# Projection and heads of a decoder layer: more q and k transfers in flight, and the first half of v issued from ScalarE's queue

## What is computed

```python
xn = _rms(x, g1)
Q = jnp.einsum('bsf,ef->bse', xn, Wq).reshape(b, s_len, H, HD)   # H = HD = 16
K, V = ...                                                        # likewise
pQ, pK = jax.nn.elu(Q), jax.nn.elu(K)
kv1 = jnp.einsum('bshe,bshd->bsed', K1, V) * SCALE
w1 = jnp.einsum('bshe,bsed->bshd', Q1, kv1)      # and w2 from the second halves
attn = w1 - lmb * w2
```

## Time and profile before

| what | value |
|---|---|
| time, median of 3 | 799.29 us (796.55 to 799.43) |
| the profiled execution | 796.2 us, its span 794.5 us |
| loop of projection and heads | about 40 to 249 us of the span |
| PE busy | 661.5 us (83%) |
| DVE, ACT, POOL busy | 494.8, 357.6, 331.8 us |

### The profile page before, as it was taken

How to read it: one execution, slowest core, us unless ns; L and a number is a source line. 1 busy time by engine, 2 the same in 40 slices (tenths; PEclk the granted TensorE clock), 3 DMA queues, 4 the chain that set the end, 5 groups by cost and what they waited for, 6 DMA issues and landing times.

```text
span 794.5 us, 22042 instructions
## 1 busy us (share of the span) xinstructions
PE 661.5 (83%) x8346; PEld 612.4 (77%) x8346; DVE 494.8 (62%) x1239; ACT 357.6 (45%) x814; POOL 331.8 (42%) x393
## 2 busy tenths in 40 slices
PE   4569879788957266766567999999999999999998
PEld 4447767576746155666447999999999999999997
DVE  4645543455421478777447877777777777777763
ACT  4343335343423344344235555555545555554432
POOL 0021110111101988887243555464555445455222
PEclk8798989898978577777858999999999999999999
DMA  8334444345332132333200011011111001110000
GB/s 267 33 61 95 101 103 121 75 121 122 92 88 83 53 106 94 115 107 100 82 20 21 21 35 34 2 35 33 33 33 33 26 7 33 33 33 14 15 14 27
DMA packets 84136, 50.08 MB, mean 63 GB/s; under 512 B 31320, under 2 KB 83808, under 8 KB 84064
## 3 DMA queue, kind: packets, MB, share of 16 engines
q1 hardware_dynamic: 84064, 49.07, 22.7%
HBM read 23.88 MB, written 12.58 MB: 46 GB/s over the span
## 4 chain that ended last, share of the span: by engine, by line
PE 48%; SPq 14%; issue 12%; DVE 10%; DMA 9%; POOL 4%; ACT 2%; POOLq 0%; DVEq 0%; ACTq 0%
PE banks L618 42%; SPq L534 9%; DMA h_qk<-p_qk 7%; PE banks L671 3%; SPq L519 2%; POOL f_hT_lo L1705 1%; DVE m_t L1374 1%; POOL m_rh L1615 1%; DVE m_at L1367 1%; DMA n_gw<-in_L_ffn_gate_w_dram 1%; DVE m_n L1361 1%; PE banks L755 1%; PE banks L781 1%; DVE m_a L1382 1%; POOL m_r L1615 1%
## 5 line engine op out<-in xcount | busy, mean ns | idle before, releaser
L1705 POOL TENSOR_TENSOR f_hT_lo<-f_hs,f_hT_hi 128x512 fp32r<-128x512 f32 x64 | 87.2, 1363 | 103.2 <-ACT f_hT_hi L1198 103.2
L1615 POOL TENSOR_TENSOR m_rh<-m_ms,mhalf 128x32 f32<-128x32 f32 x16 | 88.3, 5521 | 1.3
L1567 DVE SCALAR_TENSOR_TENSOR f_hs<-banks,nbic,f_h 128x256 f32<-128x256 f32 x128 | 54.5, 478 | 43.2 <-PE banks L618 43.2
L618 PE MATMUL banks<-woT_hi,f_hT_lo 128*128 128x256 f32 x256 | 74.5, 291 | 0.2 <-POOL f_hT_lo L1705 0.2
L618 PE MATMUL banks<-f_adT_hi,lbT_lo 128*128 128x256 f32 x256 | 72.9, 285 | 0.0
L618 PE MATMUL banks<-woT_lo,f_hT_hi 128*128 128x256 f32 x256 | 71.9, 281 | 0.0
L618 PE MATMUL banks<-woT_hi,f_hT_hi 128*128 128x256 f32 x256 | 71.7, 280 | 0.0
L618 PE MATMUL banks<-f_xT_hi,wiT_lo 128*128 128x256 f32 x256 | 71.6, 280 | 0.0
L618 PE MATMUL banks<-f_xT_lo,wiT_hi 128*128 128x256 f32 x256 | 71.6, 280 | 0.0
L618 PE MATMUL banks<-f_xT_hi,wiT_hi 128*128 128x256 f32 x256 | 71.5, 279 | 0.0
L618 PE MATMUL banks<-f_adT_lo,lbT_hi 128*128 128x256 f32 x256 | 71.5, 279 | 0.0
(11 more groups left out here) (261 smaller groups left out, 2093.4 us busy)
## 6 DMA issues: line engine op xcount, KB each, us to landing
h_qk<-p_qk SPq DMA_DIRECT2D x64, 128.0 KB, 3.7
xin<-in_x_dram SPq DMA_DIRECT2D x16, 256.0 KB, 3.6
h_v<-p_v SPq DMA_DIRECT2D x128, 32.0 KB
attn_scratch<-h_wn SPq DMA_DIRECT2D x16, 256.0 KB, 2.2
m_w<-attn_scratch SPq DMA_DIRECT2D x16, 256.0 KB, 2.7
m_x<-in_x_dram SPq DMA_DIRECT2D x16, 256.0 KB, 2.9
x_scratch<-m_y SPq DMA_DIRECT2D x16, 256.0 KB, 2.2
c_x<-x_scratch SPq DMA_DIRECT2D x16, 256.0 KB, 2.7
```

Of the source, the lines that this page charges most:

```text
L618: ins = pe.matmul(acc, left(a), right(b), start=first and n == 0, stop=last and n == 2, skip_group_check=skip)
L1567: ins = dve.scalar_tensor_tensor(out=f_hs[:, j % 2, c * T:(c + 1) * T], in0=bank[HB[j]][:, c * T:(c + 1) * T], scalar=nbic[:, f:f + 1], in ...
L1615: pool.tensor_tensor(out_ap, tmp, mhalf[:, 0:width], ALU.pow).then_inc(done, 1)
L1705: pool.tensor_tensor(lo, f_hs[:, j % 2], hi.bitcast(F32), ALU.subtract).then_inc(f_hlo, 1)
```

## The change

Three edits. The limit on q and k transfers in flight is gone. The first half of v (b = 0) is issued from ScalarE's queue, in the new stage `values_out`: four transfers between the first and the second pair of Relu and Exp, and four behind the last pair. SyncE's list is put in another order: the second half of v stands between the two halves of the input, the eight q and k transfers stand in two groups of four, and one of the two stores stands behind each group.

```diff
@@ tiles_in @@
-                    if i >= 2:
-                        sp.wait_ge(h_qkin[u.slot][i % 2], u.turn * 64 + 32 * b + 16)
-                        apart(sp)
@@ values_in @@
-                    if b == 0 and c == 0 and u.has(2):
+                    if c == 0 and u.has(2):
                         sp.wait_ge(h_ed, nth(u, ROUNDS, -ROUNDS))
@@ SyncE's list @@
-            over_all(SU, [(0, but_first_two(load_x(0))), (0, but_first_two(load_x(1))), (1, tiles_in(0, 0)),
-                          (2, values_in(1, 0)), (2, values_in(1, 1)), (1, tiles_in(0, 1)), (1, tiles_in(0, 2)), (1, tiles_in(0, 3)),
-                          (1, tiles_in(1, 0)), (1, tiles_in(1, 1)), (1, tiles_in(1, 2)), (1, tiles_in(1, 3)),
-                          (1, values_in(0, 0)), (1, values_in(0, 1)), (3, store_w(0)), (3, store_w(1))])
+            over_all(SU, [(0, but_first_two(load_x(0))), (2, values_in(1, 0)), (0, but_first_two(load_x(1))), (2, values_in(1, 1)),
+                          (1, tiles_in(0, 0)), (1, tiles_in(0, 1)), (1, tiles_in(0, 2)), (1, tiles_in(0, 3)), (3, store_w(0)),
+                          (1, tiles_in(1, 0)), (1, tiles_in(1, 1)), (1, tiles_in(1, 2)), (1, tiles_in(1, 3)), (3, store_w(1))])
@@ ScalarE @@
+            def values_out(c):
+
+                def emit(u):
+                    if u.has(2):
+                        act.wait_ge(h_ed, nth(u, ROUNDS, -ROUNDS))
+                    act.wait_ge(p_vcopy, nth(u, KD, 1))
+                    for t in range(TG):
+                        first = HT * c + t
+                        act.dma_start(h_v[first:first + HT // 2 - TG + 1:TG, u.slot].rearrange("p e n -> p (e n)"),
+                                      p_v[:, u.slot, 0, HT * (TG * c + t):HT * (TG * c + t + 1)]).then_inc(h_vin[u.slot], 16)
+                return emit
-                          (3, head_natural(3)), (1, p_values(1)), (0, p_exps(0)), (0, p_exps(1)), (0, p_exps(2)), (0, p_exps(3))])
+                          (3, head_natural(3)), (1, p_values(1)), (0, p_exps(0)), (1, values_out(0)), (0, p_exps(1)), (0, p_exps(2)), (0, p_exps(3)), (1, values_out(1))])
```

## The result

The changed kernel takes 828.02 us (median of 4, 822.04 to 830.99), the kernel before 798.5 us: a ratio of 1.037, 95% interval 1.033 to 1.041, some 29.5 us. The forecast was 803 us, with a range of 794 to 812. The profiled execution took 830.99 us; its span is 829.3.

The account below looks back on a forecast made before the run. Bound by SyncE's queue in the loop, TensorE in the tail. Step 3 starts 5.2 us earlier, step 8 3.2 later, and the loop ends 3.5 later: 799.3 + 3.5 = 802.8, said as 803 us, range 794 to 812.

Parts of the forecast that it names:

- The mechanism from step 3 on: SyncE's store waits for this step's head results and holds four k transfers; TensorE's scores wait some 4 us.
- S: Start of a loop step, its first matmul on TensorE; the prediction counted a step's terms from it.
- late v and gaps: Added to TensorE's step: 0.9 us for v landing late at `head_values(0)`, 0.5 us for issue gaps.
- the landing of k: Last of four k transfers, from issue to landing, ahead of `head_scores(0)`: taken as 3.6 us.
- the landing of v: ScalarE's last v transfers ahead of `head_values(0)`: 2.0 us of issues, then 1.9 us from the last issue.
- Steps 1 and 2: First loop steps, no store yet: windows of some 19 and 21 us, step 3 starting 5.2 us earlier.
- steps 4 to 7: Middle loop steps: 26.6 us each, wrong if under 25 or over 28 us.
- ScalarE's issue: Price of issuing one v transfer on ScalarE: taken as SyncE's 0.66 us, 2.6 us for four in a row.
- a step without a wait: Rival: the store holds nothing, all steps take 21 us, 24 us gained, 775 us; chance 0.08.
- a held clock: Rival: TensorE not slowed behind the new wait, steps 3 to 7 have 5.22 us for 6.86, 794.6 us; chance 0.12.
- the rival of two issuers that slow each other: ScalarE and SyncE issuing together: late input 808 us, dearer issues 816, or last transfer landing at 5.0, 811; chance 0.20.
- another branch: Issuers take turns, so the input's second half goes out up to 2.6 us late: 1 us a step, 808 us.

Follow-up runs that it names:

- e3: Changed kernel with both stores moved to the end of SyncE's list, no limit, v on ScalarE as changed: 811.7 us, ratio 1.018.
- e9: Changed kernel with all eight ScalarE v issues together behind the second Relu and Exp, first store still ahead of k, no limit: 811.7 us, ratio 1.021.
- e8: Changed kernel with both stores last and all eight ScalarE v issues together behind the second Relu and Exp, no limit: 785.4 us, ratio 0.984.
- e2: Changed kernel with the limit of two q and k transfers in flight put back, order and queues as changed: 832.5 us, ratio 1.039.
- e4: Changed kernel with the first half of v issued from SyncE again, first store still ahead of k, no limit: 827.1 us, ratio 1.036.
- e14: Changed kernel, both stores last, ScalarE's last four v issues moved behind the second Relu and Exp, first four as changed: 788.7 us, ratio 0.989.
- e6: Kernel before with the first half of v issued from ScalarE at the changed kernel's places, limit and SyncE order kept: 798.8 us, ratio 1.002.
- e10: Changed kernel with both stores last, all eight ScalarE v issues behind the second Relu and Exp, limit of two put back: 783.2 us, ratio 0.983.
- e1: Kernel before with only the limit on q and k transfers in flight taken out, order and queues as before: 786.0 us, ratio 0.984.
- e5: Changed kernel with both stores last and the first half of v issued from SyncE again, no limit: 785.1 us, ratio 0.983.
- e7: Changed kernel with both stores last and the limit of two put back, v on ScalarE as changed: 795.2 us, ratio 0.998.

## Why the prediction was wrong

**The mechanism from step 3 on was right.** The store holds the four k transfers in each of the six steps. Moving it to the end gives 16 us (the changed kernel against e3) or 26 (e9 against e8). Term by term in step 4, S = 126.45: the last `head_natural` ended at 136.19, 9.7 after S (predicted, with late v and gaps, 11.1). `head_scores(0)` to `head_scores(1)` took 152.24 - 145.38 = 6.86 us, as predicted, behind a wait of 6.8 us; TensorE had stood idle for these 6.8 us, and its clock was at its lower level of 1.2 GHz up to about 150.8, as this window of the changed kernel shows (columns as in the earlier trace rows):

```profile
146.00:148.00 2.00, 2.00 (x108) 1.89 (x97) 0.21 (x1) 0.00 (x0) 0.00 (x0) 0.50 0.81 226
```

**The step that failed is the landing of k.** I took 3.6 us for the last k transfer, from a step in which the limit had kept the queue short, and gave 5.0, the largest of the earlier trace rows, to a rival. It measured 6.6 in step 4: 145.38 - 138.80. Read the same way, it is 6.0 to 6.6 us in steps 3 to 7 and 6.9 in step 8, which is 2.4 to 3.3 us more than I took in each of six steps, 17 us in all. The prediction gives no reason why four transfers without a limit, issued each 0.66 us, should land as soon as under it; in a run they need 1.25 us each (e2). Of the excess of 3.0 us in step 4, some 1.7 go with ScalarE's v on the same engines in the same moment: the last k lands in 4.9 us in e4, and also in e9, where ScalarE's first v goes out only once the last k is being issued. The other 1.3 us are there without them.

**The same error a second time, in the landing of v.** I took 1.9 us from the last issue, where nothing was ahead of it. In step 2 of the changed kernel the last v issue of ScalarE began near 68.0, and `head_values(0)` started at 74.90, 6.9 us later:

```profile
60.68 8.99 SPq L516 DMA_DIRECT2D h_qk<-p_qk  x8
64.64 4.03 ACTq L1060 DMA_DIRECT2D h_v<-p_v  x4
```

The first row holds two runs: the four q transfers, issued at 0.65 us apiece from 60.68, then a wait of 3.6 us for k in `p_qk`, and the four k transfers from 66.90 on, without a limit. The last v goes out among them. ScalarE's four issues took 4.03 us in place of 2.6 because one of them, from 65.97, took 2.04; no run says why.

Steps 1 and 2, forecast at 18.9 and 21.0 us, took 22.3 (66.15 - 43.86) and 28.1 (94.27 - 66.15; v landed late). Some 2 us of step 1 lie in its mark: its first matmul came 2.0 us earlier than before, but what follows did not (the first q transfer went out at 44.88, before at 44.34). The rest is k, which landed late and held TensorE. So step 3, forecast to start at 85.7, started at 94.27, 3.4 us later than before and not 5.2 earlier. Step 3 was 32.2 against 26.0, and steps 4 to 7 took (243.53 - 126.45) / 4 = 29.3 against 26.6. The first matmul behind the loop came at 279.63, before at 248.98: 30.7 us later, which is about the difference of the medians. The two profiled executions are 34.8 us apart; the other 4 us lie behind the loop, and no run explains them.

**What was right besides, and what was not.** One reading is off without bearing on the sum: in step 1 TensorE was busy 16.3 of 22.7 us, not 21 to 22. ScalarE's issue was taken at 0.66 us and measured 0.62 to 0.65 but for a few. The first four, between the Exp, cost nothing that is clear of the noise (e14, 3.3 us above e8). VectorE's waits for the input went away. The rivals of a step without a wait and of a held clock did not occur. Of the rival of two issuers that slow each other, the branch that came is the late landing of the last of four transfers, priced there at 8 us. The rule of the Trainium skill that I had cited for another branch (Perfetto Trace Analysis, DMA Instruction, HWDGE: one descriptor generator, locked for each instruction) does not show in these times: at 137.9 to 140.5 ScalarE issued four in 2.60 us while SyncE issued its own at 0.67 us apiece, and during ScalarE's one long issue, from 65.97 to 68.01, SyncE began two, at 66.90 and 67.50.

The other rule of the Trainium skill (DMA: Bandwidth & Descriptors, Issuing engines are not separate DMA queues: a second issuer saves only issue time, all share the same engines) holds in part. e6 is flat: 5.2 us of issue time a step were taken off the bounding queue, and nothing was gained. But e10 has the limit too, and the same eight issues in the gap, and is 15 us below the kernel before. Its order of input and v differs as well, which is worth nothing between e1 and e5. So where the queue is the bound, its issue time was worth some 15 us here, once v went out early; with the limit gone (e5 against e8) the second issuer is worth nothing.

Left open: why a run of these transfers gets a third of the rate that a single one peaks at. The runs show that it needs neither the store nor ScalarE's transfers (111 GB/s from 48 to 51.2 us in e1, with q and k alone but for the last 0.2 us), and that transfers let through one by one pass at three times the rate, with idle time between them.

## What to carry to other kernels

In a queue that an engine works off in order, a wait holds what stands behind it: put a store that depends on this step's late results behind every load that this step still needs. Taking a limit on transfers in flight away helps the queue that waited (e1, 12 us) and can delay what is issued beside or behind the run (e3 against e7, 16.5 us); issue what would be late ahead of it (e8). Take a landing time only from a moment with as many transfers around it as there will be, and a rate from a run of them, never from the peak of one.

## What was not expected of the hardware

ScalarE's queue does not wait for the activation ahead of it before it issues a transfer. The changed kernel's ScalarE, at the end of step 3:

```profile
124.95 0.63 ACT L1014 ACTIVATE p_exp<-p_exp 128x512 f32<-128x512 f32 x1
125.01 2.58 ACTq L1060 DMA_DIRECT2D h_v<-p_v  x4
127.64 0.60 ACT L1036 ACTIVATE h_wT<-banks 128x512 f32<-128x512 f32 x1 [2.06 <-issue]
```

The first transfer is issued 0.06 us after the Exp starts, so four of them hold the next activation back by 2.06 to 2.13 us and not 2.6. The other surprise is the rate of q and k in a run without the limit: 107 GB/s in the changed kernel, with packets on the 16 engines for 123% of their time, against 300 at the peak of one transfer.
